# The value product of a set-attention kernel on one Trainium2 core: each step issued whole instead of in two halves

## Chip, cores and metric

The kernel runs on one core of one Trainium2 chip. The metric is device time in microseconds, the median of several runs; lower is better.

## What is computed

One transformer layer over x of shape 4 x 1024 x 128 (four batches, 1024 positions), in two parts: an attention over sums of keys and values, then a routed feed-forward part.

```python
q, k, v = split(layernorm(x) @ W_attn.T)          # 16 heads of 8
K, V = sums of k and v over dyadic sets of positions (lengths 4, 8, ..., 1024)
logits = q @ K.T * scale, masked where the set ends after t     # plus one "tail" logit
att = softmax([logits, tail]);  out = att[..., :-1] @ V + att[..., -1:] * V_tail
x = x + out @ W_proj.T
s = sigmoid(x2 @ gate_w.T); top 6 of 32 experts in the best 4 of 8 groups -> combine
x = x + einsum(relu(x2 @ up_w)**2 * combine, down_w) + shared part      # x2 = layernorm(x)
```

## The kernel before

**Batches.** The four batches run one after the other. A batch has two stages: attention (`attend`), then feed-forward (`ffn`, line numbers of both engines' loops in the listing), in which the next batch is also prepared (projections, set sums, a first share of its maxima). Between them stands no barrier; the first feed-forward matmul (L972) follows the last one of attention.

**Attention.** The 1024 queries of a batch are two windows `w` of 512, the 16 heads four groups `g` of four. 512 set columns are four chunks `c` of 128. For each (w, g) there are three kinds of work:

- max units (L871, tile `mx`): logits with queries on partitions; VectorE reduces each unit to a row maximum (L1088). `mx` has two buffers, so that unit u waits for the reduction of unit u - 2. After a group's last unit, `mfin` on VectorE and a split on GpSimd make three bf16 parts, TensorE transposes them (`mT`, L880, tile `om`), VectorE copies them to `MB` (L1095), and a transfer from SyncE's queue writes them into rows of `QA`.
- probability units (L912, tile `st`, named `exp`): logits with sets on partitions, the maximum already taken off by those rows of `QA`; ScalarE turns each unit into probabilities in `PT` (L729). `st` has two buffers of 1024 columns.
- value steps (L929, named `pv`): one for each chunk c that window w sees, 2 in window 0 and 4 in window 1 for each group, so 24 in a batch. The last step of each group covers 256 queries, the others 512. Of a step, the four heads multiply a stationary 128 x 32 block of `VA` by 128 x 512 (or 128 x 256) float32 columns of `PT`; head h writes partitions 32h to 32h + 31 of `om`. A float32 matmul is two records in the trace, so a whole step is eight records and half a step is four. After the last step ScalarE copies `om` to `OS` (`oevac`, L735), and TensorE transposes it (`oT`, L938).

The post steps of window 0 (L827 to L849 on TensorE: transposes, output projection, expert logits L843) also lie in this stage.

**What sets the order.** `attention_order()` simulates the stage once, when the program is built, with costs written out by hand, and returns `ORDER`, a list of events that all engines follow. At each turn it takes the candidate with the earliest start, then the lowest priority number. Probability units and value steps are two events each: `exp1` and `exp`, `pv1` and `pv`, half of the heads each, and other events may be put between the two. Half a value step is costed as:

```python
run(("pv1", w, g, k), start, PV_STEPS[w][k][2] * 2 * 0.47e-3, None, 0)
```

that is 0.48 us for 512 columns. In the `ORDER` of the kernel before, 10 of a batch's 24 value steps have matmuls of other lines between their halves: 7 of the 16 with 512 columns and 3 of the 8 with 256. In the other 14 the halves follow each other. In the order of the engines the names are: `mx` max units, `st` probability units, `om<-PT,VA` value steps, `om<-identb,MS` the transpose `mT`, `om<-ident,OS` the transpose `oT`.

Of the kernel before, what the change touches and what calls it, by code (L numbers as in the profile page):

```python
# [23 lines left out]
G, NG = 4, 4  # L24
# [28 lines left out]
NW, WT = T // WIN, WIN // P  # L53
# [5 lines left out]
EXP_UNITS, PV_STEPS = [[], []], [[], []]  # L59
# [59 lines left out]
def attention_order():  # L119
# [18 lines left out]
    def run(ev, start, pe, eng, t):  # L138

        order.append(ev)  # L140
        free["pe"] = start + pe
        if not eng:
            return free["pe"]
        free[eng] = max(free[eng], free["pe"] + 0.3) + t
        return free[eng]

    while maxes or exps or steps or rows or turns or post:
        now, found = free["pe"], []
        if rows and ("mfin",) + rows[0] in done:
            found.append((max(now, done[("mfin",) + rows[0]] + 0.3, free["misc"]), 0, "mT"))  # L150
        if turns:
            found.append((max(now, done[("oevac",) + turns[0]] + 0.2, free["misc"]), 1, "oT"))
        if maxes:
            u = pos_max(*maxes[0])
            found.append((max(now, ring("max", u) + 0.1 - EAGER), 3, "max"))
        if halves:
            found.append((now, 4, halves[0]))
        if steps and "pv" not in halves:
            w, g, k = steps[0]
            need = ("exp", pos_exp(w, g, PV_STEPS[w][k][3]) - 1)  # L160
            if need in done:
                before = done.get(("oevac",) + divmod(NG * w + g - 1, NG), 0.0) if k == 0 else 0.0
                found.append((max(now, done[need] + 0.1, before + 0.1), 4 + bool(halves), "pv1"))
        if exps and "exp" not in halves:
            w, g, n = exps[0]
            u = pos_exp(w, g, n)

            k = pos_pv(w, g, [x[0] for x in PV_STEPS[w]].index(EXP_UNITS[w][n][0]))
            if ("rows", w, g) in done and (k < NPT or ("pv", k - NPT) in done):
                tile = done["pv", k - NPT] if k >= NPT else 0.0  # L170
                found.append((max(now, done["rows", w, g], ring("exp", u) + 0.1, tile), 6, "exp1"))
        if post and (0, NG - 1) not in turns and ("oT", 0, NG - 1) in done:
            step = post[0]
            ready = done["post"] if "post" in done else done["oT", 0, NG - 1]
            at = max(now, ready + 0.1, last_post + POST_GAP, free["misc"] if step in MISC_STEPS else 0.0)
            found.append((at, 2, "post"))
        start, _, kind = min(found)
        if kind == "mT":
            w, g = rows.pop(0)
            free["misc"] = run(("mT", w, g, 0), start, 0.15, "dve", 0.2)  # L180
            done["rows", w, g] = free["misc"] + 3.2
        elif kind == "oT":
            w, g = turns.pop(0)
            free["misc"] = done["oT", w, g] = run(("oT", w, g, 0), start, 0.6, "dve", 0.3)
        elif kind == "max":
            w, g, n = maxes.pop(0)
            i, _, nh = MAX_UNITS[w][n]
            cols = BLK * (i + 1) * nh
            done["max", pos_max(w, g, n)] = run(("max", w, g, n), start, cols * col + 0.06 * nh, "dve", 0.06 + cols * 1.05e-3)
            if n == len(MAX_UNITS[w]) - 1:  # L190
                order.append(("mfin", w, g, 0))
                free["dve"] += 0.15
                done["mfin", w, g] = free["dve"] + 1.2
                if g == NG - 1:
                    order.append(("tail", w, 0, 0))
        elif kind == "pv1":
            w, g, k = steps[0]
            halves.append("pv")
            run(("pv1", w, g, k), start, PV_STEPS[w][k][2] * 2 * 0.47e-3, None, 0)
        elif kind == "exp1":  # L200
            halves.append("exp")
            run(("exp1",) + exps[0], start, 512 * col + 0.08, None, 0)
        elif kind == "pv":
            halves.remove("pv")
            w, g, k = steps.pop(0)
            done["pv", pos_pv(w, g, k)] = run(("pv", w, g, k), start, PV_STEPS[w][k][2] * 2 * 0.47e-3, None, 0)
            if k == len(PV_STEPS[w]) - 1:
                order.append(("oevac", w, g, 0))
                free["act"] = max(free["act"], free["pe"] + 0.1) + 0.5
                done["oevac", w, g] = free["act"]  # L210
                turns.append((w, g))
        elif kind == "exp":
            halves.remove("exp")
            w, g, n = exps.pop(0)
            _, _, nh, _, nt = EXP_UNITS[w][n]
            done["exp", pos_exp(w, g, n)] = run(("exp", w, g, n), start, 512 * col + 0.08, "act", 0.9)
        else:
            step = post.pop(0)
            pe, rest, dve = POST_TIME[step]
            order.append(("post", 0, 0, step))  # L220
            last_post = start
            if pe:
                free["pe"] = start + pe
                start = free["pe"]
            if dve:
                free["dve"] = max(free["dve"], start) + dve
                done["post"] = free["dve"] + rest - dve
            else:
                done["post"] = start + rest
            if step in MISC_STEPS:  # L230
                free["misc"] = done["post"]
# [51 lines left out]
def build(nc, x, w_qkv, w_proj, gate, e_bias, up, down, ident_c, head_sel_c, q_stair_c, k_stair_c,  # L283
# [4 lines left out]
    with ctx:  # L288
# [489 lines left out]
        def _(pe):  # L778
# [108 lines left out]
            def attend(b):  # L887
                for kind, w, g, n in ORDER:
# [4 lines left out]
                    elif kind in ("exp1", "exp"):  # L893
# [20 lines left out]
                                                start=True, stop=True)  # L914
                        if kind == "exp":
                            ins.then_inc(s_expin, 1)
                    elif kind in ("pv1", "pv"):
                        c, t0, nt, need = PV_STEPS[w][n]
                        k = pos_pv(w, g, n)
                        if kind == "pv1":  # L920
                            pe.wait_ge(s_exped, b * EXPN + pos_exp(w, g, need))
                            o = NG * w + g
                            if c == 0 and o:
                                pe.wait_ge(s_oevac, b * NW * NG + o)
                            elif c == 0:

                                pe.wait_ge(s_dev, NW * b + 1)
                        for h in half(kind, G):
                            ins = pe.matmul(opsum[32 * h:32 * h + 32, t0 - WIN * w:t0 - WIN * w + nt],  # L929
                                            VA[:, c, G * g + h, :], PT[:, k % NPT, h, 0:nt],  # L930
                                            start=(c == 0), stop=(c == 2 * w + 1), skip_group_check=True)
                        if kind == "pv":
                            ins.then_inc(s_pv, 1)
                    elif kind == "oT":
                        use_misc(b, ("oT", w, g))
                        pe.wait_ge(s_oevac, (b * NW + w) * NG + g + 1)
# [395 lines left out]
```

## Time and profile before

| | |
|---|---|
| median of 3 runs | 1023.7 us (1022.25 to 1025.47) |
| profiled execution, span of its instructions | 1027.8 us |
| TensorE busy with matmuls | 864.9 us, 84% of the span |
| VectorE, ScalarE, GpSimd busy | 518.4, 317.2, 278.3 us |
| mean granted TensorE clock | 0.815 of full |
| attention stage, four times | 119.6, 123.0, 123.0, 121.2 us |
| first feed-forward matmul of each batch | at 200.6, 450.4, 699.4, 945.0 us |

The profiled execution is one of its own, and its span is 4.1 us (0.4%) above the median of the three runs. A record's length in the timeline includes the time in which its result travels out of the array, so that a group of matmuls occupies the engine from its own start to the start of the next group, not for the length shown. The granted clock is a share of full speed: 1.00 is 2.4 GHz, 0.50 is 1.2 GHz.

### The profile page before, as it was taken

The numbers are of one execution on the slowest core, as the hardware profiler recorded it, in microseconds if no ns is written. First come the engines' busy times: TensorE is split into PE (matmuls) and PEld (weight loads), VectorE is DVE, ScalarE is ACT, GpSimd is POOL, SyncE is SP. The second block draws the span as 40 slices with busy tenths as digits, with TensorE's granted clock in tenths as the row PEclk, the third lists the DMA queues.
The fourth block names the chain that finished last, engine by engine and source line by source line (L and its number), as shares of the span: only waits on it lengthen the run. The fifth ranks groups of instructions, "written<-read, shape, count | busy, mean of one in ns | idle before, by whom it ended". The sixth has DMA issues, their size and how long they took to land.

```text
span 1027.8 us, 13052 instructions
## 1 busy us (share of the span) xinstructions
PE 864.9 (84%) x3760; PEld 379.2 (37%) x3760; DVE 518.4 (50%) x1306; ACT 317.2 (31%) x435; POOL 278.3 (27%) x384
## 2 busy tenths in 40 slices
PE   3248999887778999987887899988786999997898
PEld 1223342243434333234443333324343433333444
DVE  2524575166824566327652455724772356552653
ACT  1202343532211233442421133353231123335232
POOL 1201010145522110114462111013445310111465
PEclk9655895799968778779987887778997768769999
DMA  9650000000251000000055000000005300000000
GB/s 188 158 61 7 2 1 1 1 22 0 54 77 33 2 1 2 1 21 1 1 82 67 13 2 1 2 1 21 0 31 70 49 12 2 1 1 1 1 1 20
DMA packets 29694, 26.05 MB, mean 25 GB/s; under 512 B 3164, under 2 KB 28828, under 8 KB 29500
## 3 DMA queue, kind: packets, MB, share of 16 engines
q1 hardware_dynamic: 29628, 25.21, 14.4%
q8 instruction: 36, 0.59, 0.3%
q14 instruction: 30, 0.25, 0.1%
HBM read 18.00 MB, written 6.82 MB: 24 GB/s over the span
## 4 chain that ended last, share of the span: by engine, by line
PE 54%; issue 16%; DVE 12%; DMA 9%; POOL 5%; SPq 2%; ACT 2%; DVEq 0%; POOLq 0%; ACTq 0%
PE mx L871 16%; PE om L929 13%; PE st L912 9%; DMA QA<-q_parts 6%; PE om L991 5%; PE st L972 3%; POOL PT L656 3%; DVE PT L1239 2%; PE om L938 2%; SPq L495 1%; PE om L843 1%; PE st L980 1%; DVE XN L1041 1%; PE mx L800 1%; ACT PT L729 1%
## 5 line engine op out<-in xcount | busy, mean ns | idle before, releaser
L1088 DVE TENSOR_REDUCE MXR<-mx 128x1 f32<-128x512 f32 (+6 forms) x352 | 202.0, 591 | 250.5 <-PE mx L871 247.2
L656 POOL TENSOR_TENSOR PT<-PT 128x512 f32<-128x512 f32 x144 | 183.3, 1279 | 296.4 <-DVE PT L1239 211.7
L871 PE MATMUL mx<-KA,QA 51*128 51x448 bf16 (+5 forms) x960 | 203.4, 266 | 50.6 <-DMA QA<-q_parts 43.8
L729 ACT ACTIVATE PT<-st 128x1024 f32<-128x1024 f32 x160 | 160.1, 1022 | 219.8 <-PE st L912 219.7
L871 PEld LDWEIGHTS mx<-KA,QA 51*128 51x128 bf16 (+1 forms) x960 | 92.8, 100 | 267.1 <-issue 200.6
L929 PE MATMUL om<-PT,VA 128*32 128x512 f32 (+1 forms) x768 | 166.4, 702 | 6.4 <-ACT PT L729 6.0
L991 PE MATMUL om<-PT,wdown 128*128 128x512 f32 x288 | 158.2, 633 | 1.3 <-POOL PT L656 1.3
L757 ACT ACTIVATE PT<-st 128x512 f32<-128x512 f32 x144 | 86.0, 597 | 222.9 <-PE st L972 220.1
L912 PE MATMUL st<-QA,KA 118*128 118x256 bf16 (+2 forms) x512 | 147.8, 361 | 4.9 <-ACT PT L729 3.0
L1239 DVE TENSOR_TENSOR PT<-PT,st 128x512 f32<-128x512 f32 x128 | 86.2, 683 | 64.6 <-ACT PT L757 54.0
L972 PE MATMUL st<-XH,WUH 128*128 128x512 f32 x144 | 102.6, 713 | 0.0
L980 PE MATMUL st<-CT,exp_sel 96*128 96x512 bf16 x128 | 52.8, 413 | 45.2 <-DVE PT L1239 45.2
L912 PEld LDWEIGHTS st<-QA,KA 54*128 54x128 bf16 (+1 forms) x512 | 47.0, 102 | 85.4 <-issue 49.5
L574 POOL TENSOR_TENSOR MS<-MALL,zeros 128x16 bf16<-128x16 f32 x32 | 7.3, 229 | 244.9 <-DVE MALL L1102 244.9
L991 PEld LDWEIGHTS om<-PT,wdown 128*128 128x128 f32 x288 | 58.4, 206 | 9.0 <-POOL PT L656 3.5
L972 PE MATMUL st<-XH,WUL 128*128 128x512 f32 x144 | 61.3, 426 | 0.0
L972 PE MATMUL st<-XL,WUH 128*128 128x512 f32 x144 | 60.9, 423 | 0.0
L735 ACT ACTIVATE OS<-om 128x512 f32<-128x512 f32 x32 | 19.1, 597 | 93.9 <-PE om L929 93.9
L1117 DVE COPY ATT<-om 128x144 f32<-128x144 f32 x32 | 9.8, 305 | 75.3 <-PE om L938 75.3
L980 PEld LDWEIGHTS st<-CT,exp_sel 96*128 96x128 bf16 x128 | 13.0, 101 | 89.1 <-DVE PT L1239 68.4
L972 PEld LDWEIGHTS st<-XL,WUH 128*128 128x128 f32 x144 | 29.9, 208 | 22.3 <-issue 22.0
L972 PEld LDWEIGHTS st<-XH,WUH 128*128 128x128 f32 x144 | 29.7, 207 | 22.4 <-issue 20.5
(134 smaller groups left out, 685.2 us busy)
## 6 DMA issues: line engine op xcount, KB each, us to landing
QA<-q_parts SPq DMA_DIRECT2D x48, 128.0 KB
q_parts<-Qparts SPq DMA_DIRECT2D x8, 384.0 KB, 11.2
KA<-k_parts SPq DMA_DIRECT2D x24, 128.0 KB
X<-in_x_dram SPq DMA_DIRECT2D x4, 512.0 KB, 3.9
QA<-in_q_stair_dram SPq DMA_DIRECT2D x1, 2048.0 KB, 23.1
out_dram<-Y SPq DMA_DIRECT2D x8, 256.0 KB, 3.0
k_parts<-Kparts SPq DMA_DIRECT2D x4, 384.0 KB, 2.5
PT<-in_up_dram SPq DMA_DIRECT2D x1, 1152.0 KB, 9.5
```

What stands on the lines that cost most here:

```text
L656: pool.tensor_tensor(H[:, u % 4, :], src[:, u % 4, :], R[:, u % 4, :], ALU.mult).then_inc(s_h, 1)
L729: act.activation(PT[:, k % NPT, h0:h0 + nh, 0:nt], src, ACT.Exp, scale=SCALE).then_inc(s_exped, 1)
L757: act.activation(R[:, u % 4, :], st[:, u % 2, :], ACT.Relu).then_inc(s_relu, 1)
L871: ins = pe.matmul(mx[:, u % 2, ns * k + s0:ns * k + s1], QA[r0:K_RAW, w, h, P * (i % WT):P * (i % WT) + P], KA[r0:K_RAW, h, s0:s1], start= ...
L912: ins = pe.matmul(st[:, 2 * (u % 2) + at // WIN, at % WIN:at % WIN + a1 - a0], KA[r0:K_SUB, h, P * c:P * c + P], QA[r0:K_SUB, w, h, a0 - W ...
L929: ins = pe.matmul(opsum[32 * h:32 * h + 32, t0 - WIN * w:t0 - WIN * w + nt], VA[:, c, G * g + h, :], PT[:, k % NPT, h, 0:nt], start=(c == ...
L938: ins = pe.transpose(misc[:, P * i:P * i + P], OS[:, P * i:P * i + P], ident[:, :])
L972: ins = pe.matmul(st[:, v % 2, :], wa[:, P * k:P * k + P], xa[:, WIN * w:WIN * w + WIN], start=(n == 0), stop=(n == 2))
L980: pe.matmul(st[:, 2 + routed % 2, :], exp_sel[:, k, :], CT[:, WIN * w:WIN * w + WIN], start=True, stop=True).then_inc(s_bc, 1)
L991: pe.matmul(opsum, wdown[:, CHUNKS[n], :], H[:, d % 4, :], start=(n == 0), stop=(n == NCH - 1)).then_inc(s_dn, 1)
L1088: dve.reduce_max(MXR[:, g, i, h0:h0 + nh], mx[:, u % 2, 0:ns * nh].rearrange("p (h s) -> p h s", s=ns), AX.X).then_inc(s_maxed, 1)
L1239: dve.tensor_tensor(V[:, u % 4, :], R[:, u % 4, :], st[:, 2 + routed % 2, :], ALU.mult).then_inc(s_vw, 1)
```

## The change

A value step is one event, `pv`, and all four heads are issued together. The event `pv1` no longer exists: its waits (for the probabilities, for the output bank) stand before the whole step. Probability units keep their two halves. The planner costs a whole step at 2.0e-3 us a column plus 0.08 (1.10 us for 512 columns), and its candidate now competes with priority 4, or 5 while a probability unit is half issued.

```diff
-        if steps and "pv" not in halves:
+        if steps:
             w, g, k = steps[0]
             need = ("exp", pos_exp(w, g, PV_STEPS[w][k][3]) - 1)
             if need in done:
                 before = done.get(("oevac",) + divmod(NG * w + g - 1, NG), 0.0) if k == 0 else 0.0
-                found.append((max(now, done[need] + 0.1, before + 0.1), 4 + bool(halves), "pv1"))
+                found.append((max(now, done[need] + 0.1, before + 0.1), 4 + bool(halves), "pv"))
...
-        elif kind == "pv1":
-            w, g, k = steps[0]
-            halves.append("pv")
-            run(("pv1", w, g, k), start, PV_STEPS[w][k][2] * 2 * 0.47e-3, None, 0)
...
         elif kind == "pv":
-            halves.remove("pv")
             w, g, k = steps.pop(0)
-            done["pv", pos_pv(w, g, k)] = run(("pv", w, g, k), start, PV_STEPS[w][k][2] * 2 * 0.47e-3, None, 0)
+            done["pv", pos_pv(w, g, k)] = run(("pv", w, g, k), start, PV_STEPS[w][k][2] * 2.0e-3 + 0.08, None, 0)
...
-                    elif kind in ("pv1", "pv"):
+                    elif kind == "pv":
                         c, t0, nt, need = PV_STEPS[w][n]
                         k = pos_pv(w, g, n)
-                        if kind == "pv1":
-                            pe.wait_ge(s_exped, b * EXPN + pos_exp(w, g, need))
...
-                        for h in half(kind, G):
+                        pe.wait_ge(s_exped, b * EXPN + pos_exp(w, g, need))
...
+                        for h in range(G):
                             ins = pe.matmul(opsum[32 * h:32 * h + 32, t0 - WIN * w:t0 - WIN * w + nt],
                                             VA[:, c, G * g + h, :], PT[:, k % NPT, h, 0:nt],
                                             start=(c == 0), stop=(c == 2 * w + 1), skip_group_check=True)
-                        if kind == "pv":
-                            ins.then_inc(s_pv, 1)
+                        ins.then_inc(s_pv, 1)
```

Since the planner's costs and candidates change, the whole `ORDER` is another one. The number of matmuls on every line stays the same. Three places of TensorE's order in one batch follow. Line numbers of the changed kernel are 5 lower at L871, L880 and L912, 6 lower at L929 and 7 lower at L938.

TensorE in window 0, group 1 (the two value steps of that group), before:

```order
L929 MATMUL om<-PT,VA 32x512 x2
L858 REGISTER_ALU
L871 MATMUL mx<-KA,QA 128x384
L871 MATMUL mx<-KA,QA 128x64
L929 MATMUL om<-PT,VA 32x512 x2
...
L929 MATMUL om<-PT,VA 32x256 x2
L858 REGISTER_ALU
L871 MATMUL mx<-KA,QA 128x384
L871 MATMUL mx<-KA,QA 128x64
L929 MATMUL om<-PT,VA 32x256 x2
```

and in the changed kernel:

```order
L923 MATMUL om<-PT,VA 32x512 x4
L853 REGISTER_ALU
L866 MATMUL mx<-KA,QA 128x448
L866 MATMUL mx<-KA,QA 128x64
L853 REGISTER_ALU
L866 MATMUL mx<-KA,QA 128x384
L866 MATMUL mx<-KA,QA 128x64
L915 REGISTER_ALU
L923 MATMUL om<-PT,VA 32x256 x4
```

Four groups of value matmuls with max units between them have become two, with two max units between.

TensorE in window 1, group 0, at the second value step, before:

```order
L929 MATMUL om<-PT,VA 32x512 x2
L781 REGISTER_ALU
L878 REGISTER_ALU
L880 MATMUL om<-identb,MS 48x128
L929 MATMUL om<-PT,VA 32x512 x2
L858 REGISTER_ALU
L871 MATMUL mx<-KA,QA 128x384
```

and in the changed kernel:

```order
L866 MATMUL mx<-KA,QA 128x448
L866 MATMUL mx<-KA,QA 128x64
L915 REGISTER_ALU
L923 MATMUL om<-PT,VA 32x512 x4
L776 REGISTER_ALU
L873 REGISTER_ALU
L875 MATMUL om<-identb,MS 48x128
L907 MATMUL st<-QA,KA 128x256 x4
```

The two halves with one transpose between them are now one group with max units ahead of it and probability units behind.

TensorE in window 1, end of group 2, before:

```order
L929 MATMUL om<-PT,VA 32x256 x4
L898 REGISTER_ALU
L912 MATMUL st<-QA,KA 128x512
L781 REGISTER_ALU
L938 MATMUL om<-ident,OS 128x128 x4
L912 MATMUL st<-QA,KA 128x512 x3
```

and in the changed kernel:

```order
L923 MATMUL om<-PT,VA 32x256 x4
L776 REGISTER_ALU
L931 MATMUL om<-ident,OS 128x128 x4
L893 REGISTER_ALU
L907 MATMUL st<-QA,KA 128x512 x4
```

The transpose of the group's output now stands right behind the last value step. At the end of window 1, group 1, it has moved in the same way.

## Rows read from the trace of the kernel before

**Rows 1.** Page, part 1: busy time, share of the span, instructions.

```profile
PE 864.9 (84%) x3760; PEld 379.2 (37%) x3760; DVE 518.4 (50%) x1306; ACT 317.2 (31%) x435; POOL 278.3 (27%) x384
```

**Rows 2.** Windows, attention stages: PE, PEld, DVE, ACT, POOL busy; clock, DMA share, GB/s.

```profile
81.00:200.60 119.60, 115.48 (x571) 40.56 (x571) 58.54 (x157) 46.92 (x54) 12.79 (x34) 0.74 0.01 2
327.40:450.40 123.00, 118.87 (x580) 41.21 (x580) 59.03 (x158) 47.04 (x54) 12.79 (x34) 0.74 0.01 3
...
823.80:945.00 121.20, 115.68 (x577) 40.12 (x576) 59.58 (x159) 46.82 (x54) 13.79 (x38) 0.76 0.01 4
```

**Rows 3.** Windows of 5 us in the first attention stage, same columns.

```profile
85.00:90.00 5.00, 5.00 (x25) 2.16 (x24) 1.78 (x4) 1.31 (x2) 0.88 (x4) 0.50 0.00 0
...
105.00:110.00 5.00, 5.00 (x20) 1.07 (x18) 1.32 (x3) 0.00 (x0) 0.00 (x0) 0.64 0.01 2
```

**Rows 4.** Timeline of TensorE, first batch: start us, length us, instructions.

```profile
90.83 1.92 PE L929 MATMUL om<-PT,VA 128*32 128x512 f32 x8
93.46 1.07 PE L929 MATMUL om<-PT,VA 128*32 128x256 f32 x4
94.46 0.30 PE L880 MATMUL om<-identb,MS 128*48 128x128 bf16 x1
97.10 1.10 PE L938 MATMUL om<-ident,OS 128*128 128x128 f32 x4
...
104.03 1.92 PE L929 MATMUL om<-PT,VA 128*32 128x512 f32 x4
105.89 0.67 PE L871 MATMUL mx<-KA,QA 51*128 51x384 bf16 x2
106.49 1.92 PE L929 MATMUL om<-PT,VA 128*32 128x512 f32 x4
...
114.76 1.05 PE L929 MATMUL om<-PT,VA 128*32 128x512 f32 x4
115.74 0.76 PE L871 MATMUL mx<-KA,QA 51*128 51x256 bf16 x4
...
123.70 1.07 PE L929 MATMUL om<-PT,VA 128*32 128x512 f32 x8
124.70 0.82 PE L871 MATMUL mx<-KA,QA 51*128 51x320 bf16 x4
...
191.82 1.93 PE L929 MATMUL om<-PT,VA 128*32 128x512 f32 x8
193.69 2.34 PE L912 MATMUL st<-QA,KA 118*128 118x256 bf16 x8
...
199.85 1.09 PE L938 MATMUL om<-ident,OS 128*128 128x128 f32 x4 [0.89 <-ACT OS L735]
```

**Rows 5.** Timeline of TensorE, second batch.

```profile
338.64 1.05 PE L929 MATMUL om<-PT,VA 128*32 128x512 f32 x8
...
340.21 0.63 PE L929 MATMUL om<-PT,VA 128*32 128x256 f32 x4
340.77 0.24 PE L880 MATMUL om<-identb,MS 128*48 128x128 bf16 x1
...
342.72 0.63 PE L938 MATMUL om<-ident,OS 128*128 128x128 f32 x4
...
384.36 1.92 PE L929 MATMUL om<-PT,VA 128*32 128x512 f32 x4
386.45 1.92 PE L929 MATMUL om<-PT,VA 128*32 128x512 f32 x4
...
415.15 2.79 PE L929 MATMUL om<-PT,VA 128*32 128x512 f32 x16
```

**Rows 6.** Windows of 5 us in the second attention stage, same columns as rows 2.

```profile
385.00:390.00 5.00, 5.00 (x20) 1.49 (x16) 1.06 (x4) 0.00 (x0) 0.00 (x0) 0.65 0.01 2
415.00:420.00 5.00, 5.00 (x26) 1.71 (x25) 3.38 (x18) 1.71 (x3) 0.00 (x0) 0.50 0.00 0
```

**Rows 7.** Waits in the second attention stage: who waited for what, us, times, longest.

```profile
PEld mx L871 <- DVE MXR L1088: 6.9, 10, 1.1
```

More of the change, by code:

```diff
@@ L916, in attend @@
                             ins.then_inc(s_expin, 1)
-                    elif kind in ("pv1", "pv"):
+                    elif kind == "pv":
                         c, t0, nt, need = PV_STEPS[w][n]
                         k = pos_pv(w, g, n)
-                        if kind == "pv1":
-                            pe.wait_ge(s_exped, b * EXPN + pos_exp(w, g, need))
[L922 to L927, printed above, removed]
-                        for h in half(kind, G):
+                        pe.wait_ge(s_exped, b * EXPN + pos_exp(w, g, need))
+                        o = NG * w + g
+                        if c == 0 and o:
+                            pe.wait_ge(s_oevac, b * NW * NG + o)
+                        elif c == 0:
+                            pe.wait_ge(s_dev, NW * b + 1)
+                        for h in range(G):
                             ins = pe.matmul(opsum[32 * h:32 * h + 32, t0 - WIN * w:t0 - WIN * w + nt],
```

## The prediction

> **What bounds the kernel now.** Page first: TensorE is busy 84% of the span, VectorE half of it, the others a third or less [rows 1]. All value steps lie in the four attention stages, so I read those as windows. The reader is to see there that TensorE is busy 115.5 to 118.9 us of 119.6 to 123.0, while VectorE has about 59 and ScalarE 47 [rows 2]. In attention TensorE alone is the bound, and what its instructions occupy is what the stage costs. The four stages last 486.8 us together, 121.7 on average. (The kernel's other 541 us hold no value step, and their order doesn't change.)
>
> Then the clock column. It is 0.74 to 0.76, with only two levels, so TensorE spends about 52% of attention at 1.2 GHz: 0.52 x 0.5 + 0.48 = 0.74. It does so while it is never idle: from 85 to 90 us it is busy 5.00 of 5.00 at clock 0.50 [rows 3], and so it goes on until 108. The reader should keep this in view: a busy TensorE is not a fast one here.
>
> **What a half costs.** From the start of one group to the start of the next: a half of 512 columns takes 104.03 to 105.89, 1.86 us, at the low clock and 114.76 to 115.74, 0.98, at the full one. A whole step takes 123.70 to 124.70, 1.00 us, at the full clock and 191.82 to 193.69, 1.87, at the low one [rows 4]. Four heads take as long as two, since they write four different blocks of partitions side by side. Of 256 columns a half takes 93.46 to 94.46, 1.00, at the low clock [rows 4], and 340.21 to 340.77, 0.56, at the full one [rows 5]. So each of a batch's 10 separated steps pays one half for nothing; the 14 whose halves follow each other are already cheap and gain nothing.
>
> **Term 1, the removed halves.** At the full clock 7 x 0.98 + 3 x 0.56 = 8.5 us a batch; at the low one 7 x 1.86 + 3 x 1.00 = 16.0. In the second batch five of the seven long ones run at the low clock: 5 x 1.86 + 2 x 0.98 + 3 x 0.56 = 12.9. That is the whole gain, if nothing else moved: 4 x 12.9 = 51.6 us.
>
> **Term 2, new waits.** With less work of its own TensorE meets its partners earlier. Two transposes of the output now stand right behind the last value step and wait for ScalarE's copy of the bank; the row of that pattern shows 0.89 us [rows 4], so 1.8 for two. The max units wait for VectorE's reductions: 6.9 us over ten waits, by the weight loads, part of it covered by a running matmul [rows 7]; two max units in a row are now more frequent. Bounds: 0, since VectorE and ScalarE are under half busy, and 4.1, the idle time of the second stage as it is (123.00 - 118.87, [rows 2]), once more. I take 3 us, nearer to the upper end because of the two transposes. SyncE's transfers of maxima keep their number and order, and GpSimd's steps too; I take them as hidden, under a TensorE that is busy throughout.
>
> **Term 3, the clock.** How much does it cost? The same program place, from the second half of a batch's first value step to the transpose of that group, takes 90.83 to 97.10, 6.27 us, at the low clock in the first batch, and 338.64 to 342.72, 4.08, at the full one in the second [rows 4, 5]: a factor of 1.54 (less than 2, since weight loads and switches don't scale). The second stage has 64 us at the low and 59 at the full clock. All of it at the low clock would be 64 + 59 x 1.54 = 155 us, all at the full one 64 / 1.54 + 59 = 101. With terms 1 and 2 the changed stage would be 155 - 16 + 3 = 142 us at the low clock and 101 - 8.5 + 3 = 95 at the full one. So the change saves 13 us of 155 or 6 of 101, but the distance between the clocks is 47.
>
> What decides between them? In windows of 5 us over the four stages the clock rises 14 times within attention, twice in the first batch and four times in each other. Every time a half step that stands apart lies in the stretch just before it, and in 12 of 14 two of them with only a short unit between: 104.03 and 106.49, then the clock rises in the window 105 to 110 [rows 3, 4]; 384.36 and 386.45, then it rises in 385 to 390 [rows 5, 6]. Whole steps at the low clock did not do it: 415.15 has two of them back to back, 2.79 us, and the window shows 0.50 [rows 5, 6]; 191.82 is another. What TensorE does before a rise in attention is, nearly without a gap, value matmuls. A separated step keeps it at that for 3.7 us at the low clock, a whole one for 1.87, and then come other units. The change takes exactly those stretches away. On the other side, the falls (four in the second stage, each at a stretch of max, probability and logit matmuls) lose nothing, and such work now lies closer together.
>
> The Trainium skill, "TensorE: Matmul & The Clock Gate", section "Part 1: The HAM clock gate", says that the gate opens according to how busy the engine has been of late, and closes when it idles. By that rule alone the always busy stage would run at the full clock before and after. The trace disagrees, with 0.50 at 5.00 of 5.00 busy [rows 3].
>
> I count on one of four rises being left in a stage, since some whole steps still stand near each other (in window 1, group 2, those of 512 and 256 columns with one small transpose between). A rise bought 59 / 4 = 15 us at the full clock. 15 us at full speed do the work of 15 x 142 / 95 = 22.4 at the low one: the stage takes 142 - 22.4 + 15 = 134.6 us, 12.9 more than the 121.7 of now.
>
> **Sum.** 4 x 12.9 = 51.6 over the profiled 1027.8: 1079.4. The profiled execution stands 4.1 above the median, so against the median **1075 us**. With two rises left it would be 142 - 45 + 30 = 127 us a stage, +22 in all, 1046; with none 142, +81, 1105.
>
> **Rivals.**
> - *The clock does what it did* (faster). The gain is term 1 less term 2, 12.9 - 3 = 9.9 us a stage, so 1023.7 - 39.6 = **984**. For it: TensorE stays busy without a gap; the probability and max units are unchanged, and so are the products computed; the trace has only a few whole steps at the low clock, so that their effect on it is read from few cases. Against: the whole steps at the low clock in the trace [rows 5, 6]. It decides from the point at which a stage keeps its 48% of time at full clock. The rule of the Trainium skill above (a busy engine keeps its clock) would end here or lower; as far as the trace bears it out, it shares this rival's chance and has none beyond it.
> - *Three rises of four are left.* 142 - 67 + 45 = 119.8 us a stage, -8 in all, **1016**: the gain and the loss nearly cancel. For it: in 2 of the 14 rises only one half stood in the stretch before, beside probability units, and a whole step in such a place is as long.
> - *New waits decide.* If the full upper bound of term 2 were paid in every stage with the clock unchanged, 12.9 - 4.1 = 8.8, still a gain of 35. Waits alone don't make this change lose; only the clock does.
> - *The change does nothing*: four heads together take twice the time of two. Excluded by 1.00 against 0.98 us [rows 4], so 1 in 100 and 1024.
>
> **How the numbers follow.** A measurement of this kernel tells about 0.3% (3 us) from no change. Forecast (none, one or two rises left, 1046 to 1105): 0.75, the likeliest of it 1075. Clock as before, 984: 0.15. Three left, 1016: 0.09, with ends on both sides of 1023.7, mostly faster. Nothing: 0.01. So faster 0.21, the same 0.03, slower 0.76. The range leaves out the rival at 984 and the far end of none: 1010 to 1102. The likeliest case's own range is 1046 to 1102.
>
> **What would show it.** In the profile of the changed kernel: L923 with 192 records in each stage, in groups of eight, 1.00 or 1.87 us from start to start; TensorE idle up by 2 to 3 us a stage, most of it at the transposes L931; the mean clock of the attention stages down from 0.74 to about 0.56, and fewer than four rises in each; stages of about 135 us; the feed-forward stages with their old lengths. Wrong would be: clocks of 0.74 in the attention stages (then 984), or whole steps that cost 1.5 us and more at the full clock, or long idle times of TensorE there, or a change in the feed-forward stages, which I take to be none.

## The result and the profile after

The changed kernel takes 1093.7 us (median of four, 1079.7 to 1107.9) against 1024.6 of the kernel before beside it: a ratio of 1.058, 95% interval [1.045, 1.071]. Executions in which the clock stayed low for longer are left out of that ratio, for both kernels. The change makes the kernel slower, as predicted, by 69 us on the medians where 51 were predicted. The profiled execution took 1079.7, the shortest of the four.

Page, parts 1 and 5 of the changed kernel (compare [rows 1]):

```profile
span 1077.6 us, 13052 instructions
...
PE 918.9 (85%) x3760; PEld 392.4 (36%) x3760; DVE 519.7 (48%) x1306; ACT 319.3 (30%) x435; POOL 280.1 (26%) x384
...
L923 PE MATMUL om<-PT,VA 128*32 128x512 f32 (+1 forms) x768 | 150.1, 877 | 1.6 <-ACT PT L724 0.9
```

The value steps have the same 768 records as before, and TensorE is busy for 54 us more. Windows of the four attention stages, from the first probability unit to the first feed-forward matmul (columns as in [rows 2]):

```profile
78.22:220.79 142.57, 139.27 (x571) 46.28 (x571) 59.56 (x157) 47.59 (x54) 12.84 (x34) 0.51 0.01 1
344.86:470.60 125.74, 120.85 (x573) 40.98 (x572) 59.44 (x158) 47.24 (x54) 12.84 (x34) 0.64 0.01 2
598.45:729.06 130.61, 126.66 (x573) 42.14 (x572) 59.63 (x158) 47.34 (x54) 12.84 (x34) 0.59 0.01 1
851.72:993.67 141.95, 138.22 (x573) 45.76 (x572) 59.31 (x156) 47.49 (x54) 12.99 (x34) 0.52 0.01 3
```

They are 540.9 us together; cut in the same way, the stages of before are 119.6, 121.1, 121.1 and 119.2, or 481.0. So the whole loss lies here: 59.9 us, where the two spans differ by 49.8. VectorE and ScalarE do what they did [rows 2]. TensorE is idle for 3.3, 4.9, 4.0 and 3.7 us. What has changed is the clock, 0.51 to 0.64 instead of 0.74 to 0.76 [rows 2]. The other 10 us are a gain outside the stages; two of the feed-forward stretches of the changed kernel:

```profile
220.79:344.86 124.07, 98.50 (x373) 53.94 (x371) 69.83 (x168) 31.52 (x54) 55.94 (x59) 0.91 0.23 38
470.60:598.45 127.85, 99.50 (x374) 53.74 (x372) 70.57 (x168) 31.51 (x54) 56.47 (x59) 0.90 0.23 37
```

In the kernel before they are 128.69 us at 0.88 and 127.97 at 0.89. The second is the same; the first is 4.6 us shorter with the same instructions, at a slightly higher clock. The third is 3.7 shorter, the last 1.1 longer, and attention begins 2.8 earlier in the first batch.

The timeline of TensorE in the second stage, and windows of 5 us (the first line of them is from the first stage), show the single steps:

```profile
351.08 1.93 PE L923 MATMUL om<-PT,VA 128*32 128x512 f32 x8
352.95 1.52 PE L866 MATMUL mx<-KA,QA 51*128 51x192 bf16 x8
354.40 0.64 PE L923 MATMUL om<-PT,VA 128*32 128x256 f32 x8
354.96 0.24 PE L875 MATMUL om<-identb,MS 128*48 128x128 bf16 x1
...
358.10 1.34 PE L907 MATMUL st<-QA,KA 118*128 118x256 bf16 x6
359.28 0.91 PE L866 MATMUL mx<-KA,QA 51*128 51x448 bf16 x4
360.99 1.04 PE L907 MATMUL st<-QA,KA 118*128 118x256 bf16 x4 [0.80 <-ACT PT L724]
...
362.84 1.94 PE L923 MATMUL om<-PT,VA 128*32 128x512 f32 x8
...
406.46 1.06 PE L923 MATMUL om<-PT,VA 128*32 128x512 f32 x8
407.46 0.24 PE L875 MATMUL om<-identb,MS 128*48 128x128 bf16 x1
```

```profile
85.00:90.00 5.00, 5.00 (x30) 1.55 (x22) 1.79 (x4) 0.95 (x2) 0.88 (x4) 0.50 0.00 0
...
350.00:355.00 5.00, 5.00 (x34) 1.92 (x32) 2.44 (x5) 1.02 (x1) 0.88 (x4) 0.65 0.00 0
355.00:360.00 5.00, 5.00 (x41) 2.77 (x37) 3.43 (x10) 0.83 (x3) 0.34 (x2) 1.00 0.01 2
360.00:365.00 5.00, 4.20 (x18) 1.14 (x17) 1.91 (x4) 2.88 (x4) 1.59 (x4) 0.53 0.02 4
```

and in the kernel before:

```profile
355.00:360.00 5.00, 5.00 (x33) 2.25 (x34) 3.07 (x7) 2.64 (x3) 0.00 (x0) 1.00 0.00 0
360.00:365.00 5.00, 5.00 (x32) 1.66 (x32) 2.96 (x7) 1.62 (x2) 0.87 (x4) 1.00 0.00 0
...
400.00:405.00 5.00, 5.00 (x35) 2.75 (x27) 3.43 (x9) 0.82 (x2) 0.87 (x4) 1.00 0.00 0
405.00:410.00 5.00, 5.00 (x17) 1.31 (x18) 4.36 (x13) 2.53 (x3) 0.00 (x0) 0.56 0.01 2
```

A whole step costs 1.87 us at the low clock (351.08 to 352.95) and 1.00 at the full one (406.46 to 407.46), as forecast from [rows 4]. And here is what the prediction had thought not to happen: after one whole step at 351.08 the clock does rise (0.65, then 1.00). But it has fallen again in 360 to 365. The kernel before holds the full clock from 355 to 365 in its second stage, and there value matmuls start at 359.90, 361.58 and 362.91, with short units between; the changed kernel has none between 354.96 and 362.84, and the step at 362.84 already takes the 1.87 us of the low clock.

**How the clock is counted below.** With two levels, a stage of length L at mean clock c spends (2c - 1) x L at full speed. To three digits, from the clock records of the traces, the clocks after are 0.512, 0.640, 0.591, 0.519, that is 3.4 + 35.2 + 23.9 + 5.4 = 67.9 us of full clock in all; before they are 0.743, 0.740, 0.740, 0.758, that is 58.0 + 58.0 + 58.0 + 61.5 = 235.5. Two stages of the changed kernel with the same instructions, 142.6 us with 3.4 and 125.7 with 35.2, give the worth of a microsecond of full clock: 16.9 / 31.8 = 0.53 us of stage. This is a rough rate: the two kernels with twins below, alike in work, give (606.6 - 496.2) / (241.1 - 60.9) = 0.61, and two stages at the end of the experiments 0.66.

### The profile page after: what moved, and what is told of

Read it like the earlier page. It is cut to its first block, busy times and chain, and to the rows that moved or that the text cites. A ratio compares the mean times of both kernels' runs of the same rounds, so it can differ in the third digit from the quotient of the medians.

```text
span 1077.6 us, 13052 instructions
## 1 busy us (share of the span) xinstructions
PE 918.9 (85%) x3760; PEld 392.4 (36%) x3760; DVE 519.7 (48%) x1306; ACT 319.3 (30%) x435; POOL 280.1 (26%) x384
## 4 chain that ended last, share of the span: by engine, by line
PE 56%; issue 16%; DVE 12%; DMA 8%; POOL 5%; SPq 2%; ACT 1%; DVEq 0%; POOLq 0%; ACTq 0%
PE mx L866 17%; PE st L907 12%; PE om L923 11%; DMA QA<-q_parts 6%; PE om L984 5%; PE st L965 3%; POOL PT L651 3%; PE om L931 2%; PE om L838 2%; DVE PT L1232 2%; SPq L490 1%; DVE XN L1034 1%; PE st L973 1%; PE mx L795 1%; DMA KA<-in_k_rows_dram 1%
## 5 line engine op out<-in xcount | busy, mean ns | idle before, releaser
L866 PE MATMUL mx<-KA,QA 51*128 51x448 bf16 (+5 forms) x960 | 225.9, 293 | 49.7 <-DMA QA<-q_parts 42.0
L866 PEld LDWEIGHTS mx<-KA,QA 51*128 51x128 bf16 (+1 forms) x960 | 95.1, 103 | 280.7 <-issue 229.0
L907 PE MATMUL st<-QA,KA 118*128 118x256 bf16 (+2 forms) x512 | 179.2, 432 | 3.6 <-ACT PT L724 3.1
L984 PE MATMUL om<-PT,wdown 128*128 128x512 f32 x288 | 154.9, 621 | 1.3 <-POOL PT L651 1.3
L923 PE MATMUL om<-PT,VA 128*32 128x512 f32 (+1 forms) x768 | 150.1, 877 | 1.6 <-ACT PT L724 0.9
L907 PEld LDWEIGHTS st<-QA,KA 54*128 54x128 bf16 (+1 forms) x512 | 49.7, 110 | 91.8 <-issue 61.2
L973 PEld LDWEIGHTS st<-CT,exp_sel 96*128 96x128 bf16 x128 | 12.9, 101 | 88.3 <-DVE PT L1232 66.8
L931 PE MATMUL om<-ident,OS 128*128 128x128 f32 x128 | 30.1, 380 | 10.4 <-ACT OS L730 10.4
```

Of the source, the lines that this page charges most:

```text
L866: ins = pe.matmul(mx[:, u % 2, ns * k + s0:ns * k + s1], QA[r0:K_RAW, w, h, P * (i % WT):P * (i % WT) + P], KA[r0:K_RAW, h, s0:s1], start= ...
L907: ins = pe.matmul(st[:, 2 * (u % 2) + at // WIN, at % WIN:at % WIN + a1 - a0], KA[r0:K_SUB, h, P * c:P * c + P], QA[r0:K_SUB, w, h, a0 - W ...
L931: ins = pe.transpose(misc[:, P * i:P * i + P], OS[:, P * i:P * i + P], ident[:, :])
L973: pe.matmul(st[:, 2 + routed % 2, :], exp_sel[:, k, :], CT[:, WIN * w:WIN * w + WIN], start=True, stop=True).then_inc(s_bc, 1)
L984: pe.matmul(opsum, wdown[:, CHUNKS[n], :], H[:, d % 4, :], start=(n == 0), stop=(n == NCH - 1)).then_inc(s_dn, 1)
```

## The experiments

The question after the result: is it the clock, and what takes it away? Theory A: the separated halves, matmuls over all 128 rows of the array ("full-height" below), kept the clock up, and their removal costs it, whatever the order. Theory B: the new order does it (other neighbours, other waits). Theory C: TensorE is no longer busy enough. The table has all runs; the medians of before are those taken beside each run. "Stages" is the sum of the four attention stages in the profiled execution, "full" what of it ran at the full clock, "idle" the stages less TensorE's busy time, all in us. These three columns come from one execution each, and it is not always a typical one: it is the longest of its kernel for the old order with whole steps, for the new order with halves and for both variants in pairs, and the shortest for the change. The comparisons were made on different chips.

| kernel | median us (range) | before | ratio, 95% | stages | full | idle |
|---|---|---|---|---|---|---|
| before | 1024.6 | | | 481.0 | 235.5 | 17 |
| the change | 1093.7 (1080 to 1108) | 1024.6 | 1.058 [1.045, 1.071] | 540.9 | 67.9 | 16 |
| zero twins, 128 rows | 1035.8 (1034 to 1039) | 1015.2 | 1.025 [1.019, 1.030] | 496.2 | 241 | 21 |
| zero twins, 64 rows | 1156.4 (1148 to 1158) | 1015.2 | 1.144 [1.141, 1.147] | 606.6 | 61 | 15 |
| old order, whole steps | 1059.0 (1050 to 1065) | 1015.2 | 1.044 [1.036, 1.053] | 523.8 | 70 | 11 |
| new order, halves | 1057.0 (1035 to 1074) | 1015.2 | 1.028 [1.018, 1.039] | 528.1 | 203 | 23 |
| whole steps in pairs, retuned | 1030.3 (1012 to 1038) | 1035.2 | 1.005 [0.981, 1.028] | 500.8 | 114 | 13 |
| whole steps in pairs | 1033.4 (1018 to 1038) | 1035.2 | 1.012 [0.995, 1.030] | 494.9 | 133 | 19 |
| the change again | 1099.1 (1085 to 1114) | 1035.2 | 1.076 [1.058, 1.093] | 549.0 | 55 | 16 |
| an order for the clock | 917.0 (913 to 951) | 1024.0 | | 374.6 | 251 | 5 |
| that order again | 926.3 (918 to 972) | 1030.2 | 0.906 [0.886, 0.927] | 392.5 | 228 | 8 |
| that order, halves apart | 945.1 (935 to 955) | 1030.2 | 0.934 [0.915, 0.954] | 395.1 | 282 | 6 |

### Useless work put back: twins of 128 and of 64 rows

Ten steps of a batch, seven of 512 columns and three of 256, are followed by four matmuls of the same shape whose stationary block is zeros, added to the same bank; the output doesn't change. The order stays that of the changed kernel. In the second variant the twins use 64 of the array's rows. All edits here are against the changed kernel.

```diff
+TWINS = {(0, 0, 0), (0, 0, 1), (0, 1, 0), (0, 1, 1), (0, 2, 0), (0, 2, 1), (1, 0, 0), (1, 0, 1), (1, 1, 1), (1, 2, 0)}
...
+                        for h in range(G if (w, g, n) in TWINS else 0):
+                            ins = pe.matmul(opsum[32 * h:32 * h + 32, t0 - WIN * w:t0 - WIN * w + nt],
+                                            zeros[0:128, 0:32], PT[0:128, k % NPT, h, 0:nt],
+                                            start=False, stop=(c == 2 * w + 1), skip_group_check=True)
```

(64 rows: `zeros[0:64, 0:32], PT[0:64, ...]`. The value step's own `stop` is left to its twin.)

> The changed kernel and its order, but in each batch the ten value steps that stood in separated halves before are followed at once by a second group of four float32 matmuls of the same size whose stationary block is zeros (they add 0 to the output). So the work that the change removed is back as useless work, 12.9 us a stage at the clocks of before, 8.5 if all at the full one, 16 if all at the low one. Theory clock (the time was lost since the stretches of unbroken value matmuls before each rise are gone): those stretches are back, three to four rises a stage return, attention's clock goes from about 0.57 back to 0.70 to 0.76, and the kernel is faster than the changed one in spite of the work: 1030 to 1070 us. Theory waits and order (the new order of max and probability units costs the time, the clock is a by-product): the work adds to the changed kernel's 1080 to 1094 us: 1130 to 1150 us.

> As the zero twins, but the extra matmuls use only 64 rows of the array (zeros[0:64], PT[0:64]): same columns, same number, same time each. Theory clock, in the form that it is long value matmuls over all 128 rows that go before a rise, and that max units with 51 rows don't do it: no more rises than in the changed kernel (clock of attention 0.50 to 0.60), and the work comes on top: 1120 to 1165 us. If any busy stretch of long matmuls raised the clock, it would be as the full-height twins, 1030 to 1070 us. Theory waits and order: 1130 to 1150 us for both, so the pair of runs decides.

With full-height twins the kernel takes 1036 us: 58 less than the changed kernel, for 160 matmuls (320 records) more (ten steps of a batch: 7 x 1.00 + 3 x 0.56 = 8.7 us at full speed, 35 over four batches). With half-height twins it takes 1156, 63 more than the changed kernel. Number, columns, places and waits of the twins are the same in both; only the rows differ. Both times, and all clocks but one (0.61 in the first stage of the half-height twins), lie where theory A had put them. Two stages of each:

```profile
79.17:203.81 124.64, 119.74 (x651) 42.40 (x651) 58.03 (x157) 47.05 (x54) 12.80 (x34) 0.74 0.01 2
327.61:451.85 124.24, 118.27 (x652) 42.86 (x652) 58.58 (x158) 46.94 (x54) 12.79 (x34) 0.75 0.01 2
```

and with 64 rows:

```profile
350.03:504.34 154.31, 150.20 (x653) 45.66 (x652) 60.04 (x158) 47.59 (x54) 12.84 (x34) 0.54 0.01 1
629.71:785.41 155.70, 152.40 (x653) 47.42 (x652) 59.79 (x158) 47.60 (x54) 12.84 (x34) 0.53 0.01 1
```

The reader is to see the same 652 instructions with a clock of 0.75 in one and 0.54 in the other, the slower one being the busier (150.20 of 154.31 against 118.27 of 124.24). That ends theory C. The timeline of the full-height twins shows a rise as it happens:

```profile
98.20 1.94 PE L924 MATMUL om<-PT,VA 128*32 128x512 f32 x8
99.91 1.44 PE L928 MATMUL om<-PT,zeros 128*32 128x512 f32 x8
101.28 0.90 PE L867 MATMUL mx<-KA,QA 51*128 51x448 bf16 x4
102.11 0.64 PE L924 MATMUL om<-PT,VA 128*32 128x256 f32 x8
```

Step and twin are 16 records of 128 rows and take 3.08 us, where two steps take 3.74 at the low clock and 2.00 at the full one: the clock rises within them, and what follows runs at the full one.

The full-height twins also give the price of the new order at an equal clock. They put ten groups of value matmuls a batch back beside the steps that had been separated, and have 241 us of full clock where before has 235: their stages are 496.2 us long against 481.0, 15 us more (4 of them idle time), and their median is 21 us above that of before on the same chip.

### The two halves of the change, one at a time

*Old order, whole steps.* The planner costs and orders as before; of its list the second half of each step is dropped and the first issues the whole. *New order, halves.* The planner is the changed one; 8 of a batch's 24 steps are split around the max unit that follows them, the others are issued as two halves in a row.

```diff
-ORDER = attention_order()
+ORDER = [("pv",) + e[1:] if e[0] == "pv1" else e for e in attention_order() if e[0] != "pv"]
```

```diff
+def apart(order):
...
+        if e[0] == "pv":
+            out += [("pv1",) + e[1:], nxt, e] if nxt[0] == "max" else [("pv1",) + e[1:], e]
+            i += 1 + (nxt[0] == "max")
...
+ORDER = apart(attention_order())
```

> The order of the kernel before, with each value step issued whole at the place of its first half; nothing else moved. This does the first part of the change alone. Theory clock: the removed halves (8.5 to 16 us a stage) are gained and the rises are partly lost; attention's clock between the two kernels, 0.60 to 0.70, time 1000 to 1060 us. Theory that the new order of the other units is what costs: here the order is the old one, so the whole gain of 40 to 50 us shows, 975 to 985 us. Theory that whole issue alone costs all of it: as the changed kernel, 1080 us and more.

> The order of the changed kernel, but each value step that has a max unit behind it (8 of 24 in a batch) is in two halves again with that max unit between them; the others stay whole. More work than the changed kernel by 8 to 15 us a stage. Theory clock: the separated halves make long stretches again, clock 0.65 to 0.72, the time 1040 to 1075 us, below the changed kernel in spite of the work. Theory waits and order: 1120 to 1140 us.

The old order with whole steps is 4.4% slower than before (1059 us is the end of the expected 1000 to 1060, and its clocks of 0.55 to 0.59 lie below the expected 0.60 to 0.70). So the removal of the halves takes most of the clock away by itself. In the profiled executions its stages have 70 us of full clock, hardly more than the change's 68; but that pairs its longest execution with the change's shortest. The mean clock of every execution is on record, and over the whole kernel its four have 487 to 532 us at the full clock, the change's ten 431 to 483, so that the new order takes some clock too. Splitting 8 steps again in the new order brings 203 us of the 235 back, and 37 us of time (1057.0 against 1093.7, on two chips), as expected, though it adds work.

Theory A stands, and B has a smaller part. On the medians of that chip the whole steps alone cost 44 us, and the new order, with the twins, 21 at an unchanged clock. The two add up to 65, and the change costs 69 in the result and 64 in its repetition, on other chips. Carried to a stage without any full clock (length plus 0.53 us for each us at full) the stages of before are 151.4 us on average, those of the old order with whole steps 140.2, those of the change 144.2, and with full-height twins 156.0: the new order costs 4 to 5 us a stage both times. Of the 4 between the two kernels of whole steps, 1.3 are idle time; what the rest is was not tried.

### Whole steps in pairs

If a rise needs a longer stretch of value matmuls, two whole steps in a row should give it without redundant work. A step with an even number now waits for the probabilities of its successor too, and value steps get priority 1. The first of the two variants also has other costs in the planner (a column of a whole step 1.5e-3, of VectorE and ScalarE 0.6e-3, a post step later).

```diff
-            if need in done:
+            both = len(steps) > 1 and k % 2 == 0
+            last = ("exp", pos_exp(w, g, PV_STEPS[w][k + 1][3]) - 1) if both else need
+            if need in done and last in done:
                 before = done.get(("oevac",) + divmod(NG * w + g - 1, NG), 0.0) if k == 0 else 0.0
-                found.append((max(now, done[need] + 0.1, before + 0.1), 4 + bool(halves), "pv"))
+                found.append((max(now, done[last] + 0.1, before + 0.1), 1 + bool(halves), "pv"))
```

> Whole value steps, but two at a time: an even step waits in the planner until the probabilities of the next one are there too, and value steps get priority 1; the planner's costs are set to 1.5e-3 us a column for a value step, 0.6e-3 for the other matmuls, 1.1 for an exp, and post steps get priority 6.5. No useless work: the same matmuls as the changed kernel. Two whole steps in a row are 2.8 to 3.7 us of unbroken value matmuls at the low clock, as long as a separated step was. Theory clock: the rises are back (attention's clock 0.66 to 0.76) and the removed halves are gained as well: 985 to 1020 us, level with or faster than the kernel before. Theory that whole steps as such can't hold the clock: 0.55 to 0.60 and 1050 to 1090 us.

> The pairing and priority 1 of the retuned pairs, with the costs and all else of the changed kernel. Theory clock: most of it is the pairing, so at least half of the way from the changed kernel back: attention's clock 0.62 to 0.70, 1020 to 1055 us. If the pairing did nothing and the costs all: 1075 us and more.

> The changed kernel once more, timed in the same rounds as the pairs: 1065 to 1105 us, ratio to the kernel before 1.04 to 1.08, clock of attention 0.50 to 0.64, with a spread of more than 2% between executions since the clock's rises fall differently.

Pairs bring the time back to that of before, 1030 and 1033 beside 1035, and on the same chip the change takes 1099. The interval of each includes a ratio of 1. The full clock is at 114 and 133 us, half of before's 235, and the work saved pays for the rest. The retuned pairs had been expected at 985 to 1020 us and clocks of 0.66 to 0.76; their clocks are 0.60 to 0.62, so the length of the stretch alone does not bring the clock of before back. That the retuned costs do anything beside the pairs can't be told: 3 us between medians, with 26 and 19 us between the executions of either.

### An order made for the clock

The planner's result is replaced by a list that was written out by hand: first many max units (they run at the low clock), then two whole value steps in a row, and from there max units and halves of probability units in turn, with a value step between them every few microseconds. The work is that of the changed kernel. In the string M is a max unit, E and e the halves of a probability unit, V a whole value step, m, O and P transposes and post steps.

```diff
-ORDER = attention_order()
+PLAN = ("MMeMMMmEMMMMeMMEeEmMVVMeMEMeMEMOMeMEMmVMeMEMeMVMMEMOeMEMVMeMEMmeMVMEMOMeMEM"
...
+ORDER = replay(PLAN)
```

> Whole value steps and the same matmuls as the changed kernel, in an order of attention written out by hand as a string of letters (one for each event) instead of the planner's: value steps of the first window stand in pairs or with one or two short units between, those of the second lie spread so that no long stretch is without one, and fewer events change between kinds of matmul. Theory clock: if the order is what holds or loses the clock, an order made for it beats both kernels: attention's clock 0.70 to 0.85, stages of 95 to 108 us instead of 121 and 135, the kernel 935 to 985 us. If whole steps can't hold the clock as separated ones do, 0.60 and below, 1010 to 1040 us as the pairs.

> The order made for the clock, but 6 of a batch's 24 whole steps (all of 512 columns) are in two halves again with the max unit that follows them between. At an attention clock of 0.80 and more a half costs close to 0.98 us: 4 x 6 x 0.98 = 24 us more than that order with whole steps, up to 45 us if they fall at the low clock. Theory clock: where the clock is held anyway, separated halves only cost: 940 to 965 us, attention's clock within 0.03 of the other. If separated halves helped here too, 915 us or less.

> The order made for the clock once more, on the same chip as the run with its halves apart: 910 to 935 us, attention's clock 0.80 to 0.87, and 20 to 45 us below that run.

It takes 917 us, 10% less than the kernel before, and less than the 935 to 985 that were expected. The slowest of the order's six executions, 951, lies below the fastest of before's eleven, 998. The second comparison has 0.906 [0.886, 0.927]. It beats both kernels. Two of its stages, and a piece from the beginning of the second one, with two windows cut at the same places:

```profile
80.47:176.29 95.82, 94.93 (x572) 37.81 (x572) 58.64 (x156) 46.76 (x54) 12.89 (x34) 0.81 0.01 2
301.97:395.12 93.15, 92.23 (x573) 36.71 (x573) 59.92 (x158) 46.76 (x54) 12.88 (x34) 0.84 0.01 2
```

```profile
311.76 1.69 PE L938 MATMUL st<-QA,KA 118*128 118x256 bf16 x6
313.39 0.30 PE L906 MATMUL om<-identb,MS 128*48 128x128 bf16 x1
313.62 0.39 PE L897 MATMUL mx<-KA,QA 115*128 115x64 bf16 x4
313.94 2.27 PE L954 MATMUL om<-PT,VA 128*32 128x512 f32 x16
316.14 0.49 PE L897 MATMUL mx<-KA,QA 51*128 51x448 bf16 x2
316.48 0.49 PE L938 MATMUL st<-QA,KA 118*128 118x256 bf16 x2
316.80 0.49 PE L897 MATMUL mx<-KA,QA 51*128 51x448 bf16 x2
317.12 0.49 PE L938 MATMUL st<-QA,KA 118*128 118x256 bf16 x2
```

```profile
313.94:315.61 1.67, 1.67 (x12) 0.40 (x13) 0.98 (x4) 0.83 (x2) 0.46 (x2) 0.52 0.02 6
315.61:316.14 0.53, 0.53 (x12) 0.12 (x4) 0.00 (x0) 0.00 (x0) 0.39 (x2) 1.00 0.02 5
```

With 92 us busy of 93 TensorE has become faster without having less to do. The pair at 313.94 is a step of 512 columns and one of 256 (the timeline merges them into one line): the first takes 1.67 us, nearly all of it at the low clock, the second 0.53 at the full one. So here too the rise lies behind a whole step. Behind the pair, max units (whose long matmul uses 51 rows) and halves of probability units (118 rows) take turns of 0.33 us.

The clock is not shown to be all of the gain. The stages are 166 us shorter than the change's and have 183 us more of full clock: at 0.53 to 0.66 us each that is 97 to 121, and 11 are idle time, which leaves 34 to 58 unexplained. The rate itself depends on what runs at the full clock (a value half saves 0.88 us there, 1.86 less 0.98, for its 0.98), so part of the rest can still be the clock's. Fewer changes between kinds of matmul, which the order had also been written for, are no cause: in the trace TensorE goes from one line to another 603 times in these stages and 511 times in the change's.

With the halves set apart again in that order (6 steps of a batch, around a max unit) the kernel takes 945 us instead of 926 on the same chip, or 917 on another: its stages have more full clock, 282 us, and are longer all the same. Its 945 lie in the expected 940 to 965, and the 19 us between the medians are near the 24 x 0.98 = 24 us that its separated halves occupy at the full clock: where the clock is held already, a separated half costs about what it occupies. The repetition shows how loosely the clock is held even so (a stage at 0.67, where 0.80 to 0.87 had been expected):

```profile
298.33:410.62 112.29, 109.50 (x573) 38.90 (x573) 60.75 (x158) 46.94 (x54) 12.88 (x34) 0.67 0.01 2
538.07:630.99 92.92, 90.20 (x574) 36.48 (x573) 59.83 (x158) 46.71 (x54) 12.89 (x34) 0.86 0.01 2
```

These are two stages of one execution with the same instructions, 19 us apart, with 37 and 67 us of full clock (19.4 / 29.2 = 0.66).

## Why the prediction was right, and where it was not

**What bounds the kernel: right.** TensorE is busy 525.0 of the 540.9 us of attention, and its idle time stays between 5 and 23 us in the stages of all kernels, while their length goes from 375 to 607.

**Cost of a step: right.** 1.87 and 1.00 us, 0.56 for 256 columns at the full clock (354.40 to 354.96). The rival "the change does nothing" is out.

**Term 1, the removed halves, 12.9 us a stage (16 at the low clock): too large for the change as it was made.** In stages carried to the low clock the term is 16. At 0.53 us for each microsecond of full clock, 151.4 less 140.2 gives 11.2 with the old order and 7.2 with the change's own; at 0.61 it is 14.6 and 10.6. So it is nearly right for the old order, and the new one takes back some 4 us a stage. The prediction had let the new order cost nothing but waits; beyond 1.3 us of idle time, what it costs is open.

**Term 2, new waits, 3 us a stage: wrong, it is about 0.** TensorE's idle time in the stages went from 17 to 16 us in all. The transposes do wait where they were expected to; the waits of the second stage after and before:

```profile
PE om L931 <- ACT OS L730: 2.7, 3, 0.9
...
PEld mx L866 <- DVE MXR L1081: 3.3, 9, 0.8
```

```profile
PE om L938 <- ACT OS L735: 1.5, 2, 0.9
```

That is 1.2 us more for the transposes, but 3.6 less at the weight loads of max units ([rows 7] has 6.9). The term was reckoned as if the clock stayed; a TensorE at the lower clock meets its partners later, not earlier, which fits these rows but was not tested by itself.

**Term 3, the clock: right in its size, wrong in its parts.** The forecast was one rise of four left, each with 15 us of full clock, so 60 us in all; measured are 67.9. The prediction had called a change in the feed-forward stages a sign of being wrong: two of four keep their old lengths, two are 4.6 and 3.7 us shorter, for a reason that was not looked for. The factor 1.54 between the clocks is 1.53 by the two stages above (1.61 to 1.66 by the other pairs), and the forecast of 142 us for a stage wholly at the low clock met one of 142.6. But there are 11 rises in the changed kernel's attention, not 4 (one, five, three and two in the stages), against 14 before: they last 6.2 us on average instead of 16.8. The sentence "Whole steps at the low clock did not do it" is the step that fell: 351.08 is a whole step, and the clock rose behind it, and in the trace all 11 rises come behind, or near the end of, a whole step of 512 columns that began at the low clock; there are 60 such steps. The two cases that the sentence was read from ([rows 5], 415.15, which is a step of 512 columns and one of 256, and 191.82) were too few. Nor did separated halves always raise it: those at 87.22 and 90.83 in the kernel before were followed by the low clock until 108. So the removed halves had both raised the clock and kept it up. Before there was one rise for each 17.5 us at the low clock (245.5 us, 14 rises), after only one for each 43 (473.0 us, 11 rises), and what a rise won was kept for a shorter time. How a fall comes earlier was looked at in one place only: before the fall at 360 in the second stage TensorE did six probability matmuls and four of max units and was idle for 0.80 us, where the kernel before has its value matmuls of 359.90 to 363.46. Which of these it was, the idle time or the missing value matmuls, that place can't tell; the kernel before falls without any idle time (405 to 410).

**The sum: partly luck.** The stages are 59.9 us longer. At 0.53 that is (235.5 - 67.9) x 0.53 = 88.8 us lost by the clock and 28.8 saved in work (4 x 7.2); at 0.61 it is 102 and 42. These parts add up by the way they are worked out, and are no test of the rate. The prediction had 91 lost by the clock (4 x 22.8, from 134.6 = 121.7 - 12.9 + 3 + 22.8), 12 by waits and 52 saved. So the clock was about right, the waits 12 too many and the work saved 10 to 23 too large, and the last two errors cancel in part. Further, 10 us that nobody had foreseen were gained outside the stages, and bring the 59.9 down to 49.8, near the 51.6 of the forecast. 1075 lies 5 us below the profiled 1080 and 19 below the median of 1094. The prediction had taken 0.3% for the scatter of a measurement; one profiled execution of this kernel is no median.

**The rivals.** *The clock does what it did* (984) is refuted by 0.51 to 0.64. *Three rises left* (1016) had no stage of its kind: the shortest, the second at 125.7 us with 35.2 at the full clock, is that of two rises left (127 us with 30). *Waits decide* is out, with 16 us of idle time where there were 17. Of busyness as the rule: the Trainium skill, "TensorE: Matmul & The Clock Gate", section "Part 1: The HAM clock gate", says that the gate is set "based on how busy the PE has been recently". Here the measurement differs: the busier kernel (592 of 607 us, twins of 64 rows) has 61 us of full clock, the less busy one (475 of 496, twins of 128 rows) has 241. The height of the matmuls counts (the twins), and beside it which units follow one another (the order made for the clock). How the chip weighs them was not measured.

## What to carry to other kernels

Before a redundant matmul is taken out of a stretch that TensorE bounds, read the granted clock of that stretch in short windows: if it goes up and down while TensorE is never idle, the order and the height of the matmuls can decide the clock, as they did here, and "less work" can be slower. Then look for an order that spreads the full-height matmuls before trimming them; here order and trimming together were worth 10%, and trimming without it cost 6%. Take several executions before a per cent is believed.

## What the runs showed of the hardware

- Zeros times probabilities in 128 rows raise the clock as real value steps do (0.75 against 0.64 in the second stage); the same in 64 rows does not (0.54).
- TensorE fell from 2.4 to 1.2 GHz while busy 5.00 of 5.00 us (the kernel before, 1.00 in 400 to 405 us, 0.56 in 405 to 410), and stayed at 1.2 at 5.00 of 5.00 (85 to 90 us, in the kernel before and after).
- With one core, the same program and the same chip, executions scatter by up to 5%: the kernel before took 1003.1 to 1055.1 us beside the repetition of the change, and that 1084.7 to 1113.6 (2.7%). The same stage of the same instructions took 142.6 or 125.7 us within one execution. The same section of the Trainium skill says that the moment of a rise shifts from run to run. The traces agree in so far as one and the same stage holds the clock differently: the second stage of the changed kernel has 35.2 us of full clock in one profiled execution and 6.8 in the other. No run here shows how much of the 17 us is due to such a shift.
- Weight loads follow the clock only in part: 111 ns (median) in the kernel before, for the blocks of probability units between 81 and 108 us, at the low clock, and 96 between 110 and 152, at the full one; 142 and 108 for the value blocks. So the prediction's reason for a factor below 2 holds in part.
